# Turning layer 0's rows on VectorE in blocks of 32, with the tables in edge order

## What is computed

```python
# layer 0
e_feat = concatenate([x[src], x[dst], edge_attr])       # 96 features an edge
v = relu(e_feat @ W1 + b1) @ W2 + b2                    # 64 hidden, 32 out
x = layernorm(x + maximum(segment_max(v, dst), x))
# layer 1
msg = einsum(w_comp[type], x[src], weight)              # 16 bases
a = tanh(relu(sum((x[src] @ A1 + b) * (x[dst] @ A2 + b + rel_emb[type])) / sqrt(32)))
nei = segment_sum(a * msg, dst)
x = layernorm(x + relu(where(in_deg > 0, nei + x[src[last_edge]] @ self_w, 0)))
```

## Time and profile before

| | |
|---|---|
| median of 3 runs | 4339.46 us (4338.24 to 4342.36) |
| profiled execution, its own time | 4343.61 us |
| its span, first to last instruction | 4341.8 us |
| busy in the span | PE 3907.0, DVE 3122.2, ACT 903.0, POOL 3217.8 us |
| layer 0 | from 284.49 us (first source transposes) to 1911.93 (first gather of maxima) |
| layer 1 | to about 4100 us |

### The profile page before, as it was taken

How to read it: one execution, slowest core, us unless ns; L and a number is a source line. 1 busy time by engine, 2 the same in 40 slices (tenths; PEclk the granted TensorE clock), 3 DMA queues, 4 the chain that set the end, 5 groups by cost and what they waited for, 6 DMA issues and landing times.

```text
span 4341.8 us, 76892 instructions
## 1 busy us (share of the span) xinstructions
PE 3907.0 (90%) x23347; PEld 1771.7 (41%) x23347; DVE 3122.2 (72%) x5125; ACT 903.0 (21%) x1615; POOL 3217.8 (74%) x3330
## 2 busy tenths in 40 slices
PE   7989999999999999932989999999999999999941
PEld 3444554555455455411533333333333333333311
DVE  7856666666666666526678888888888888888844
ACT  4401111111111111110022222222222222222211
POOL 7767777777777777767777777777777777777745
PEclk9999999999999999965999999999999999999975
DMA  8123333333333333324145555555555555555511
GB/s 340 29 77 105 92 99 98 92 98 98 93 98 98 94 97 98 111 63 76 29 129 140 136 143 137 137 141 136 140 139 135 143 138 138 142 136 138 140 45 32
DMA packets 411406, 494.42 MB, mean 114 GB/s; under 512 B 165363, under 2 KB 314448, under 8 KB 409008
## 3 DMA queue, kind: packets, MB, share of 16 engines
q1 hardware_dynamic: 274800, 278.43, 25.1%
q0 software_dynamic: 106432, 131.97, 13.5%
q10 hardware_dynamic: 29952, 81.80, 5.0%
HBM read 345.09 MB, written 146.77 MB: 113 GB/s over the span
## 4 chain that ended last, share of the span: by engine, by line
PE 38%; DMA 8%; issue 5%; DVE 3%; POOL 1%; DVEq 0%; ACT 0%; POOLq 0%; ACTq 0%
PE psum L1589 8%; PE psum L1513 8%; PE psum L1522 8%; PE psum L1578 4%; DMA xg<-h_dram,src_idx 4%; PE psum L1676 3%; DMA last_rows<-sum_rows,last_i 2%; PE psum L1598 2%; DMA early<-max_rows,last_i 2%; PE psum L1551 1%; PE psum L1530 1%; DVE late L1254 1%; PE psum L1414 1%; PE psum L1575 1%; PE psum L1539 1%
## 5 line engine op out<-in xcount | busy, mean ns | idle before, releaser
L691 POOL DMA_INDIRECT xg<-h_dram,src_idx x1540 | 1502.7, 976 | 481.2 <-DMA xg<-h_dram,src_idx 345.3
L691 POOL DMA_INDIRECT xg<-in_x_dram,src_idx x1392 | 1328.7, 955 | 435.6 <-DMA xg<-in_x_dram,src_idx 306.4
L1254 DVE TENSOR_TENSOR late<-late,psum 128x512 f32<-128x512 f32 x1664 | 1080.0, 681 | 231.0 <-PE psum L1513 191.3
L1428 PE MATMUL psum<-early,late 128*128 128x448 bf16 x5712 | 1131.4, 354 | 9.5 <-DVE late L1051 7.4
L1428 PEld LDWEIGHTS psum<-early,late 128*128 128x128 bf16 x5712 | 545.0, 98 | 628.3 <-issue 115.9
L1513 PE MATMUL psum<-comp,sel 128*128 128x512 bf16 x1664 | 587.1, 384 | 42.1 <-DVE late L1254 41.5
L1522 PE MATMUL psum<-late,basis 128*32 128x512 f32 x3328 | 446.0, 608 | 0.0
L1589 PE MATMUL psum<-x,late 128*128 128x448 bf16 x1344 | 380.6, 353 | 0.0
L1051 DVE TENSOR_TENSOR late<-psum,lane_hot 128x448 f32<-128x448 f32 x272 | 169.7, 624 | 289.1 <-PE psum L1428 275.0
L1159 DVE TENSOR_TENSOR_SCAN scan<-fresh,scan,psum 128x512 f32<-128x512 bf16 x103 | 131.8, 1280 | 326.4 <-PE psum L1474 326.2
L1513 PEld LDWEIGHTS psum<-comp,sel 128*128 128x128 bf16 x1664 | 154.9, 98 | 493.5 <-DVE late L1254 299.3
(11 more groups left out here) (159 smaller groups left out, 4424.7 us busy)
## 6 DMA issues: line engine op xcount, KB each, us to landing
sp_in<-spread SPq DMA_DIRECT2D x208, 256.0 KB, 3.7
late<-type_dram SPq DMA_DIRECT2D x104, 512.0 KB
sum_rows<-early ACTq DMA_DIRECT2D x104, 512.0 KB
spread<-late SPq DMA_DIRECT2D x16, 1664.0 KB
ea<-in_edge_t SPq DMA_DIRECT2D x104, 256.0 KB
keep<-keep_dram SPq DMA_DIRECT2D x832, 32.0 KB
max_rows<-out ACTq DMA_DIRECT2D x104, 256.0 KB, 2.1
xg<-h_dram,src_idx POOLq DMA_INDIRECT x1540
```

Source lines behind the costliest of these rows:

```text
L691: pool.indirect_dma_start(out=out, out_offset=None, in_=table, in_offset=bass.IndirectOffsetOnAxis(ap=index, axis=0), engine_sem=pool_issu ...
L1254: dve.tensor_tensor(prod[:, n % G_BUFS, :], x4[:, s.slot(2), g, :], bank[C_BANK[n]][:, :], ALU.mult).then_inc(prod_ready, 1)
L1428: last_ = pe.matmul(hot_bank[tile_slot(s, t)], class_hot[s.slot(2)][:, HOT - hot_tiles(s) + t, c, :], x_parts[:, c, q, :], start=c == 0 an ...
```

## The change

The three tables are laid out by edge: row n is edge n, and `table_row` goes. In layer 0 a partition loads 16 consecutive edges of one stream (4 loads of 32 partitions), so that 32 x 32 blocks can be transposed within each stream's 32 partitions: VectorE transposes the spread rows into PSUM (`spread_blocks`) and the scanned maxima into `out0` (`out_blocks`), from which ScalarE issues 4 stores. TensorE's `spread_turn` and `scan_turn` and ScalarE's eviction leave layer 0. `out_blocks` stands after the pick of tile 1, `spread_blocks` at the head of VectorE's step. In layer 1 the rows are turned as before, on TensorE; the load now collects them from the four streams' places in rows of 128 bytes, and the store writes 1 KB per stream and partition. From step 8 on three tiles are picked for every step, and one for each of the last five.

```diff
-HOTS = (2, 3, 3, 3)
+FIRST_HOTS = (2, 3, 3, 3, 2, 3, 3, 3)
...
-    return HOTS[n % len(HOTS)] if n < FEW_HOT else 0
+    return FIRST_HOTS[n] if n < PRE else HOT if n < FEW_HOT else 1
...
-    return s.i * tiles_of_round(s.unroll) + tiles_of_round(s.off) + t
+    return sum(FIRST_HOTS) + (s.at - PRE) * HOT + t
...
+        sp_cols = sp_in[:, :, :, :].rearrange("p u k f -> p u (k f)")
...
-        out0 = sb("out0", [P, 2, SLOTS, F])
+        out0 = sb("out0", [P, 2, LEN])
...
-        spread_v = spread[0:EDGES, :].rearrange("(s p k) f -> s p k f", s=STEPS, p=P)
-        spread_heads = spread[0:STREAMS, :]
-        max_v = max_rows.rearrange("(s p k) f -> s p k f", s=STEPS, p=P)
-        sum_v = sum_rows.rearrange("(s p k) f -> s p k f", s=STEPS, p=P)
+        spread_v = spread[0:EDGES, :].rearrange("(g s e k) f -> s g e (k f)", g=STREAMS, s=STEPS, e=F)
+        max_v = max_rows.rearrange("(g s e k) f -> s g e (k f)", g=STREAMS, s=STEPS, e=F)
+        spread_w = spread[0:EDGES, :].rearrange("(g s p j) f -> s p j g f", g=STREAMS, s=STEPS, p=P)
+        sum_v = sum_rows.rearrange("(g s p j) f -> s p g (j f)", g=STREAMS, s=STEPS, p=P)
...
-                sp.dma_start(sp_in[:, s.slot(2)], spread_v[s.at]).then_inc(spread_in[0][s.slot(2)], 16)
+                for g in range(STREAMS):
+                    sp.dma_start(sp_cols[F * g:F * g + F, s.slot(2)], spread_v[s.at][g]
+                                 ).then_inc(spread_in[0][s.slot(2)], 16)
...
-                sp.dma_start(sp_in[:, s.slot(2)], spread_v[s.at]).then_inc(spread_in[1][s.slot(2)], 16)
+                sp.dma_start(sp_in[:, s.slot(2)].rearrange("p (j g) f -> p j g f", g=STREAMS), spread_w[s.at]
+                             ).then_inc(spread_in[1][s.slot(2)], 16)
...
-                wait_step(act, s, o_turned[0])
-                wait_out(act, s, stored[0])
-                act.copy(out0[:, u].rearrange("p k f -> p (k f)"), bank[5][:, :]).then_inc(o_ready[0], 1)
-                store(0, s, out0[:, u], max_v)
+                wait_step(act, s, o_ready[0])
+                for g in range(STREAMS):
+                    act.dma_start(max_v[s.at][g], out0[F * g:F * g + F, u, :]).then_inc(stored[0][u], 16)
...
-                act.copy(out1[s.slot(4)][:, :, 0:F], bank[4][:, :].rearrange("p (k f) -> p k f", f=F)
-                         ).then_inc(o_ready[1], 1)
+                act.copy(out1[s.slot(4)][:, :, :, 0:F], bank[4][:, :].rearrange(
+                    "p (j g f) -> p g j f", g=STREAMS, f=F)).then_inc(o_ready[1], 1)
...
-                table_row(begin, row, a, b)
-                link(dve.tensor_tensor(row, row, spare, ALU.subtract))
+                link(dve.tensor_tensor(row, begin, spare, ALU.subtract))
...
-            table_row(last[:, :], place[:, :], 0, NODE_COLS)
-            link(dve.tensor_copy(last_i[:, :], place[:, :]))
+            link(dve.tensor_copy(last_i[:, :], last[:, :]))
...
+            def by_edge(columns):
+
+                return columns.rearrange("p (e k) -> p k e", e=F)
+
+            def spread_blocks(s):
+
+                wait_in(dve, s, spread_in[0], 16 * STREAMS)
+                wait_step(dve, s, d_ready[0], lag=1)
+                dve.transpose(by_edge(bank[1][:, :]), sp_cols[:, s.slot(2), :].rearrange(
+                    "p (k f) -> p k f", f=F)).then_inc(s_turned[0], 1)
+
+            def spread_scan0(s):
+
+                u = s.slot(2)
+                wait_step(dve, s, hid_done, each=2, lag=2)
+                wait_step(dve, s, s_turned[0])
+                dve.tensor_tensor_scan(dt_[:, u, :], keep[:, s.slot(4), :], bank[1][:, :], before(s, dt_),
+                                       ALU.mult, ALU.add).then_inc(d_ready[0], 1)
+
+            def out_blocks(s):
+
+                wait_step(dve, s, scanned[0])
+                wait_out(dve, s, stored[0], 16 * STREAMS)
+                dve.transpose(out0[:, s.slot(2), :].rearrange("p (k f) -> p k f", f=F),
+                              by_edge(scan[:, s.slot(2), :])).then_inc(o_ready[0], 1)
...
             def step0(s):
                 u = s.slot(2)
-                wait_step(dve, s, hid_done, each=2, lag=2)
-                spread_scan(0, s, 1)
+                spread_blocks(s)
+                wait_in(dve, s, keep_in[0], 16 * STREAMS)
...
+                spread_scan0(s)
                 if hot(s.plus(3)):
                     build_hot(s.plus(3))
...
-                wait_step(dve, s, o_turned[0], lag=2)
+                wait_step(dve, s, o_ready[0], lag=2)
...
                     for t in range(1, hot_tiles(n)):
                         pick_tile(n, t)
+                        if t == 1:
+                            out_blocks(s)
+                if not pe_picks(n) or hot_tiles(n) == 1:
+                    out_blocks(s)
...
                 source_turn0(s)
-                wait_step(pe, s, d_ready[0], lag=1)
-                spread_turn(0, s, 1)
...
                     pick_products(n, pieces[1], hot_tiles(n) * CLASSES)
-                scan_turn(0, s, 5)
```

More of the change, by code:

```diff
@@ L445, in gathered0 @@
         def gathered0(s, use):
-            hots = HOTS[s.slot(PRE) % len(HOTS)]
-            return s.earlier(PRE) * 16 * (SLOTS - hots) + use * 16 * (SLOTS - hot_tiles(s))
+            first = FIRST_HOTS[s.slot(PRE)]
+            if s.known and s.earlier(PRE) == 0:
+                return use * 16 * (SLOTS - first)
+            return (s.earlier(PRE) - 1) * 16 * (SLOTS - HOT) + use * 16 * (SLOTS - hot_tiles(s)) + 16 * (SLOTS - first)
         def hot(s):
@@ L510, in border_rows @@
         def border_rows(eng, table, n):
-            ends = table[EDGES - STREAMS:EDGES, 0:F]
+            ends = table.rearrange("(g n) f -> g n f", g=STREAMS)[:, STREAM - 1, 0:F]
             eng.dma_start(border[:, :, :], ends.partition_broadcast(P)).then_inc(border_in[n], 16)
@@ L760, in _ @@
             for u in range(2):
[L761 removed]
+                pool.wait_ge(stored[0][u], 16 * STREAMS * (STEPS // 2))
             for c in range(CHUNKS):
@@ L960, in count @@
                                       ).then_inc(dve_counted, 1)
-            def table_row(edge, out, a, b):
-                link(dve.tensor_scalar(out, edge, float(STREAMS), None, ALU.mult))
-                for g in range(1, STREAMS):
-                    link(dve.tensor_scalar(past[:, a:b], edge, float(g * STREAM), float(1 - EDGES), ALU.is_ge,
-                                           ALU.mult))
-                    link(dve.tensor_tensor(out, out, past[:, a:b], ALU.add))
             def place_nodes(a, b):
```

37 lines of the change are left out of this document (17 added, 20 removed).

## The result

The changed kernel takes **4382.01 us** (median of four runs, 4380.08 to 4384.67) where the kernel before takes 4339.51: a ratio of 1.0097, 95% interval 1.0080 to 1.0115. It is slower by 1.0%, clear of the spread of either kernel's runs; 4334.5 was forecast, with 4350 as the upper end. The profiled execution has a span of 4379.2 us against 4341.8: **37.4 us** have to be found.

What follows compares the result with a forecast made beforehand. Layer 0 was taken as TensorE's for 91 steps and GpSimd's in the last three, layer 1 as equally tight. 9.4 - 17.9 - 0.4 + 4 = -4.9 us against the profiled 4341.8; 4334.5 us from the median, range 4316 to 4350.

Steps and rivals of the forecast that it cites:

- The steps with picks: Layer 0, steps with tiles picked: transposes leave TensorE (81.9 us), third tiles add 91.3 us, net +9.4 us; 16.36 a step.
- the -1.7 of step 6: Layer 0, step 6: sources turned before the scan and picks covering the copy give 1.7 us back.
- The wait that takes the place of the one removed: Layer 0's short steps: ScalarE's copy of the next step is late behind this step's stores; 1.0 us more a round.
- 2.94 + 3.5 + 3.71 = 10.1 us: Layer 0, round without picks: to scan end, to first-layer products, back to second layer; 1.0 us more, +5.0 over five.
- four steps with one tile (10.1 + 0.3 ...): End of layer 0, after step 97: six pick products replace a 0.9 us wait; with two empty steps 61.8 us.
- the gain of 17.9: End of layer 0, step 97's sources to the gathers of the maxima: 75.9 us instead of 93.8.
- The loop's code: VectorE's layer-0 loop: longer code may be fetched anew at 10 back edges; 0 to 15 us, taken as +4.
- the forecast cover of 2.1 us: Layer 0, steps with picks: scanned rows ready at 4.2 us, wanted at 6.3, so VectorE's transposes cost no time.
- Layer 1's loop gets shorter stalls: Rival, VectorE's layer-1 loop: code lying elsewhere allows about 0.9 us a pass, 22 passes, 4315 us; chance 0.08.
- The five new tiles here fill time in which TensorE waited: Last five steps of layer 0: one tile each goes into TensorE's waits, within the 17.9 us gain there.
- The slower case: Rival, layer 1: small packets delay gathers' landing; +20 us, 4355, at 0.2 us a step, at most +184; chance 0.10.
- The whole gain is eaten in layer 0: Rival, layer 0: full 3.7 us loads at every back edge (+15 for +4) and transposes of 1.07: 4347; chance 0.20.

Runs made afterwards that it cites:

- e5: Changed kernel with ScalarE's four stores after the next source's copy and, in the last five steps, VectorE's scan before the tile: 4327.73 us, kernel before 4346.54.
- e16: Changed kernel with 64 one-column fills put before layer 1 on VectorE: 4359.52 us, kernel before 4339.54.
- e15: Changed kernel with late stores, scan first, two tiles in one step of eight, three in others, none in the last five: 4319.24 us, kernel before 4344.86.
- e14: Changed kernel with the old tile counts (2, 3, 3, 3 a step, none in the last five): 4336.96 us, kernel before 4340.09.
- e3: Changed kernel with layer 1's spread rows loaded in 2 KB pieces, in wrong order: ratio 0.9823, 0.9819, once 0.985 to the kernel before, on slower chips only.
- e17: Changed kernel, late stores, scan first, two tiles in one step of eight and in each of the last five, 64 fills: ratio 0.9775, slower chips only.

## Why the prediction was wrong

**Right.** The steps with picks: 16.36 us apart, TensorE without a gap, +10.0 us against +9.4; the -1.7 of step 6 doesn't show. The block transposes, 1.03 and 0.72 us against 0.85 each; that they and the stores are covered in steps with picks. Layer 1's small packets: DMA share 0.64 as forecast, 0 us in the steady passes. The wait that takes the place of the one removed, ScalarE's copy behind four stores: named, and sized within 0.1 us (3.6 against 3.5). TensorE no longer waits for a gather at the end. The operations before layer 0: -7.6 against -3.7, of which 2.7 went to step 0's wait for its loads.

**The step that failed is "2.94 + 3.5 + 3.71 = 10.1 us"**, a round without picks, in its last term. 12.6 were measured over five of them. The first two terms held (2.9 and 3.6). The 3.71 was read from a round in which TensorE waits 0.85 to 1.4 us and keeps the full clock, and carried into one in which it waits 4.3, though the wait of 3.5 stood in the same sum. After that wait the clock is granted at the lower level and the 3.71 are 6.15. A wait was priced by its own length and not by what it does to the engine that waits. Five rounds at 2.4 us are the 12.0 us that steps 1 to 5 miss. The same term stands in the six rounds at the end, where it measured 5.4 to 6.9 us: another 13 to 14 us. e5, with the stores behind the copy, has rounds of 8.3 us, mostly at full clock.

**The second, and as large, is "four steps with one tile (10.1 + 0.3 ...)"**. The term put the six products of a tile into TensorE's wait, without following VectorE's queue: the tile's mask stands before the scan and waits for nine more products that come after the second layer's. That makes the scan 3.4 us late, in steps 97 to 101: 17 us. The four steps measured 15.9 us each in place of 10.4 (+21.8), the two after them 27.9 in place of 20.2 (+7.7), and the drain held (6.2 against 6.6): 105.0 in place of 75.9, the 29.1 us. With the same count of tiles and the two orders changed the tail was 69.2 us, so the gain of 17.9 was there to be had, and more.

**The loop's code.** Taken at +4, half of 8. A pass of layer 0's loop on VectorE is 301 instructions, as counted, and is fetched anew each time (116 packets between 400 and 1800 us against 15, and 23.3 us of idle before L1130), but the forecast cover of 2.1 us holds it: steps 6 to 96 take 16.37 us each where 16.36 was forecast. For layer 1 the rival "Layer 1's loop gets shorter stalls" had the mechanism right and gave 0.9 us a pass; this kernel's code happened to fall where it is still fetched. e16 moved it and got 0.94 a pass.

**"The five new tiles here fill time in which TensorE waited"**: in line with e15, which lacks them and has TensorE wait 59 us for GpSimd, though it also lacks tiles in the loop; in the changed kernel hidden behind the order of VectorE.

**The rivals.** The slower case was placed in layer 1's packets; the loss came from the seams. "The whole gain is eaten in layer 0" had the place and neither the cause nor the size: it needed late fetches and transposes of 1.07 us, and neither cost time in the steps with picks.

**Open.** The 4.0 us between the first gather of the maxima and the end. They arise before layer 1's loop: from that gather to the first branch of VectorE's layer-1 loop it is 571.3 us before, 575.2 after, 575.3 to 576.3 in e5, e15 and e16, and 570.6 in e14, which has the small packets as well. The theory of e3, gathers that land late behind small packets, isn't borne out: by the packets of GpSimd's queue (32 a gather, taken in order, an estimate), of the gathers of sources between 2200 and 2525 us 118 of 253 landed more than 3.2 us after their start before the change and 113 of 246 after it. The run with large packets was only had on the other chips. Not tried on a chip of the first kind: e17, which should unite the gains; the late stores alone; the scan first alone; the new counts alone.

## What to carry to other kernels

Price a removed or added wait together with the clock of the engine that waits: four microseconds of idle on TensorE made the next three groups of products 1.7 to 1.9 times as long, and the average table of stages showed nothing of it. When work moves from one engine to another, look at the steps at the seams first: in the steady steps every queue had cover, while the 13 steps at the two ends of layer 0 became 31 us longer, of a net loss of 37. Follow each engine's queue there, and not only the engine that sets the pace: a mask in front of a scan cost 3.4 us a step. Issue transfers behind the copy that the next engine waits for, not before it. The kernel with that and the scan put first takes 4327.73 us where the kernel before took 4346.54; the turns alone gave 3 us in one execution, and by the estimate above only because VectorE's code had moved. Before a small gain or loss is put down to an edit, see whether a loop has come to be fetched anew, or ceased to be.

## What the runs showed of the hardware

- A 128x512 block transpose of float on VectorE took 0.72 us with its output strided in PSUM and 1.03 us with its input strided in SBUF. Four stores of 64 KB held ScalarE's queue for 1.75 to 1.86 us.
- TensorE's granted clock was at the lower level for two to three groups of products after a wait of 4.3 us (0.59 as a mean over 6.1 us). In the kernel before it fell after waits of 1.38 and 1.40 us (0.67 over 10.3 us), and in e5, with waits of 0.7 to 1.2 us, in two rounds of five. From 284 to 331 us, mostly short steps, the mean was 1.00 before, 0.79 after and 0.91 in e5.
- A loop of 291 instructions on VectorE was fetched again at each pass (3.4 us idle, 5 to 6 packets a pass) or not at all, by 64 instructions put in front of it: 0.9 us a pass, 20 us over 21 passes.
- On some chips the kernel before took 5986 to 6065 us, 38 to 40% more than on the others, with the same durations of the instructions looked at and late starts after waits.
